# TensorE's order inside a unit of the first attention: score, logit, value products or piece, score, logit, rest

## The reference, cut to what matters

```
x_norm = layer_norm(x, g1, beta1)
q, k, v = x_norm @ Wq + bq, x_norm @ Wk + bk, x_norm @ Wv + bv     # 16 heads of 8
q, k = apply_rope(q) / sqrt(8), apply_rope(k)
attn = softmax(q @ k.T);  out = attn @ v                            # per head, 512 x 512
x = x + out @ Wo + bo
x = x + relu(layer_norm(x, g2, beta2) @ W1 + b1) @ W2 + b2
```

## Time and profile before

| | |
|---|---|
| median of 3 runs | 1780.76 us (1778.65 to 1782.49) |
| span of the profiled execution | 1776.1 us |
| around the span, from the median | 4.7 us |
| mean granted TensorE clock | 0.912 |
| PE / PEld / DVE / ACT / POOL busy | 82% / 54% / 72% / 53% / 39% of the span |
| first attention, main loop | 54.7 to about 604 us |

### The profile page before, as it was taken

One profiled execution on the slowest core, in us unless ns is written; L12 is line 12 of the kernel. 1 busy time (PEld: TensorE's weight loads), 2 busy tenths in 40 slices (PEclk: granted clock), 3 DMA queues, 4 the chain that ended last, 5 costly groups with the idle time before them and its releaser, 6 DMA issues. The chain is left out here.

```text
span 1776.1 us, 37567 instructions
## 1 busy us (share of the span) xinstructions
PE 1455.7 (82%) x11726; PEld 964.8 (54%) x11726; DVE 1274.7 (72%) x3482; ACT 935.2 (53%) x1914; POOL 694.1 (39%) x812
## 2 busy tenths in 40 slices
PE   3999999999999729995378887878888887837993
PEld 1224334333343319994256766666666665627993
DVE  6777888888787435555777879697978786834555
ACT  2577777777775505662435455454545453314561
POOL 3122342633520334554233344444444541233552
PEclk8699999999998969997689999898999998978997
DMA  6211111111110332222544443434344434132225
GB/s 158 66 42 59 47 52 53 61 53 49 49 62 15 128 123 67 73 72 82 164 150 126 126 128 106 131 109 129 112 125 122 130 111 138 38 130 56 71 72 162
DMA packets 122418, 166.37 MB, mean 94 GB/s; under 512 B 21490, under 2 KB 96018, under 8 KB 121586
## 3 DMA queue, kind: packets, MB, share of 16 engines
q1 hardware_dynamic: 113330, 145.69, 28.1%
q0 software_dynamic: 8896, 18.30, 3.0%
HBM read 116.04 MB, written 47.60 MB: 92 GB/s over the span
## 5 line engine op out<-in xcount | busy, mean ns | idle before, releaser
L1124 DVE TENSOR_REDUCE a_M<-a_F 128x1 f32<-128x512 f32 x512 | 325.8, 683 | 90.0 <-PE a_F L1318 88.1
L1025 ACT ACTIVATE L_W<-a_ST 128x512 f32<-128x512 f32 x512 | 276.8, 595 | 89.1 <-PE a_ST L1359 88.3
L2028 ACT ACTIVATE L_W<-c_ST 128x1024 f32<-128x1024 f32 x160 | 163.3, 1021 | 188.4 <-PE c_ST L2408 141.1
L2630 ACT ACTIVATE L_hT<-L_P,L_W1s 128x128 f32<-128x128 f32 x600 | 171.5, 368 | 142.9 <-PE L_P L2711 110.6
L2616 POOL DMA_INDIRECT L_yd<-L_ys,L_di x150 | 163.1, 1087 | 151.6 <-DVE L_ys L2662 147.2
L489 POOL DMA_INDIRECT L_xd<-L_XN,L_place_i x128 | 124.4, 972 | 146.5 <-issue 131.9
L1359 PE MATMUL a_ST<-L_W 74*128 74x512 bf16 x512 | 168.9, 395 | 11.1 <-ACT L_W L1025 6.3
L1318 PE MATMUL a_F<-L_W 72*128 72x512 bf16 x512 | 167.1, 403 | 7.7 <-DVE a_M L1124 6.9
L2702 PE MATMUL L_P<-L_xT,L_W1s 128*128 128x128 f32 x1200 | 161.0, 278 | 0.0
L2711 PE MATMUL L_P<-L_W,L_hT 128*128 x1200 | 159.1, 276 | 0.1
L2407 PE MATMUL c_ST<-ident,c_SD 128*128 128x128 f32 x512 | 149.7, 292 | 5.5 <-ACT L_W L2028 5.5
(11 more groups left out here) (430 smaller groups left out, 3164.9 us busy)
## 6 DMA issues: line engine op xcount, KB each, us to landing
c_QS<-c_q SPq DMA_DIRECT2D x32, 504.0 KB
c_QS<-c_rd SPq DMA_DIRECT2D x32, 378.0 KB
L_xg<-L_xd SPq DMA_DIRECT2D x150, 64.5 KB
L_W<-a_q SPq DMA_DIRECT2D x32, 288.0 KB
L_W<-a_k SPq DMA_DIRECT2D x96, 96.0 KB
L_W<-c_k SPq DMA_DIRECT2D x96, 96.0 KB
L_W<-in_L_w SPq DMA_DIRECT2D x8, 1024.0 KB
c_QI<-c_r SPq DMA_DIRECT2D x32, 216.0 KB
```

What stands on the lines that cost most here:

```text
L1025: act.activation(PT[:, j, kk, :], ST[:, kk, :], ACT.Exp).then_inc(sem(exped), 1)
L1124: dve.tensor_reduce(M[:, t, h:h + 1], FB[n % BANKS][:, :], AX_X, ALU.max).then_inc(sem(maxed), 1)
L2028: act.activation(PT[:, j, :, :], ST[:, :, :], ACT.Exp).then_inc(sem(exped), 1)
L2630: act.activation(hT[:, n % 2, f, :], PS[2 + 2 * (n % 2) + f // 2][:, (f % 2) * P:(f % 2 + 1) * P], func, bias=W1s[:, n % WB, F + f:F + f + ...
```

## The change

Inside a unit TensorE's order was: score, score, [turn_max], logit, logit, [value products], [piece], [turn_values]. It becomes: score, logit, then the value products where the unit has them and the piece where it has none, score, logit, [turn_max], [the piece, in a unit that has value products], [turn_values]. `scores` issues one score instead of two. No instruction is added or removed, and the orders of ScalarE, VectorE, GpSimd and the DMA queues stay.

```
-            def scores(i, g, j):
+            def scores(i, g, j, kk):
...
-                if j == 0:
+                if j == 0 and kk == 0:
                     pe.wait_ge(*turn(mstacked, i, 32 * (g + 1)))
-                for kk in range(2):
-                    kt = 2 * w + kk
-                    pe.wait_ge(*turn(exped, i, 2 * (UQ * g + j) + kk - 1))
-                    pe.matmul(ST[:, kk, :], KS[0:KR0, h, kt * P:(kt + 1) * P], QS[0:KR0, h, :],
-                              start=True, stop=True).then_inc(sem(scored), 1)
+                kt = 2 * w + kk
+                pe.wait_ge(*turn(exped, i, 2 * (UQ * g + j) + kk - 1))
+                pe.matmul(ST[:, kk, :], KS[0:KR0, h, kt * P:(kt + 1) * P], QS[0:KR0, h, :],
+                          start=True, stop=True).then_inc(sem(scored), 1)
...
-                        scores(i, g, j)
+                        b, ns = ahead(i, g, j, n1) or (i, [])
+                        uses = pieces(u, tail, n1, n2, routed)
+                        valued_here = j in (5, 6) or (j in (1, 2) and (g or tail))
+                        scores(i, g, j, 0)
+                        for n in ns[0:1]:
+                            logits(b, n)
+                        if j in (1, 2) and g:
+                            values(i, g - 1, j + 1)
+                        elif j in (1, 2) and tail:
+                            values(i - 1, NQ - 1, j + 1)
+                        elif j in (5, 6):
+                            values(i, g, j - 5)
+                        else:
+                            for use in uses:
+                                piece(use, i, prev)
+                        scores(i, g, j, 1)
+                        for n in ns[1:2]:
+                            logits(b, n)
                         if j == 5 and has_quad(g, 1, n1):
                             turn_max(*next_quad(i, g))
-                        if ahead(i, g, j, n1):
-                            b, ns = ahead(i, g, j, n1)
-                            for n in ns:
-                                logits(b, n)
-                        if j in (1, 2):
-                            if g:
-                                values(i, g - 1, j + 1)
-                            elif tail:
-                                values(i - 1, NQ - 1, j + 1)
-                        if j in (5, 6):
-                            values(i, g, j - 5)
-                        for use in pieces(u, tail, n1, n2, routed):
-                            piece(use, i, prev)
+                        if valued_here:
+                            for use in uses:
+                                piece(use, i, prev)
```

## The result

The kernel after takes 1801.42 us, the median of 4 runs (1796.91 to 1813.03), where the kernel before took 1780.34 (1778.65 to 1782.49, 4 runs): a ratio of 1.0159, 95% interval 1.0102 to 1.0216. It is slower. The forecast was 1795, with a range of 1779 to 1812.

The account below looks back on a forecast made before the run. TensorE was taken to set the main loop's pace (busy 528.6 of 550 us), with short waits behind ScalarE and VectorE. Full batches, joints and batch 0 summed to +13.8 us on 1780.8, giving 1795, range 1779 to 1812.

Parts of the forecast that it names:

- pieces behind each other: Consecutive piece units: next piece waits for ScalarE's copy behind the second exponential; +0.64 units 15/16, +0.70 units 7/8.
- The +0.8 of units 31 and 0: Batch joint: the piece wait between units 31 and 0, claimed to cost 0.8 us.
- the normalisations: Later second exponential delays minus_max and XN by 0.68: net +0.42 from unit 21; YN +0.1, ZN -0.15.
- the joint: Between batches: second logits come later, so two 0.65 us waits for VectorE's maxima go, 1.3 us saved.
- units 19 and 20: Piece wait for ScalarE's copy, with turn_values between as partial cover: +0.28 us per full batch.
- units 2 to 4 at nothing: Units 2, 3, 4: extra waits and units 4 and 5's losses taken as 0, bounds -0.1 and +0.4.
- Batch 0: First batch, almost without pieces: 3.3 lost at quad joints, 1.1 and 1.2 gained, net +1.0 us.
- The landing of the quad's maxima: Later turn_max makes the maxima's DMAs land late in batch 0: 1.1 us at three quad joints, 3.3.
- The runs with less wait: Batch 0, five runs of units without value products or piece: spread scores avoid 0.2 us waits, estimated -1.1.
- the two waits for maxima: Batch 0: two waits for maxima like those at the batch joint were to go, -1.2 us.
- The clock, the rival of 0.14: Piece waits bring more 1.2 GHz stretches: 36 us more, 1831, or 1813 with half; chance 0.14.
- The faster case: Spread scores keep ScalarE from falling behind; all waits but the piece pairs' 2.9 go: 1771 us; chance 0.10.

Follow-up runs that it names:

- e3: Changed kernel, but ScalarE copies the piece of a unit without value products between that unit's two exponentials; 1830.93 us, ratio 1.0060 to the kernel before.
- e1: Changed kernel with every piece put back behind the second logit, value products staying between the pairs; 1826.9 us, ratio 1.0031 to the kernel before.
- e2: Changed kernel with units that have value products ordered as in the kernel before, pieces still moved in the others; 1852.56 us, ratio 1.0185 to the kernel before.
- e5: e3 plus ScalarE's quad-maxima copy, XN and YN between exponentials, and TensorE's turn_max directly behind the first logit; 1782.29 us, ratio 1.0066 to the kernel before.
- e6: e5 plus VectorE's other work of a unit between its two maxima; 1766.68 us, ratio 0.9942 to the kernel before; again 1762.39 us, 0.9924.
- f1: Changed kernel with only VectorE's edit of e6, its other work of a unit between the two maxima; 1836.97 us, ratio 1.0138 to the kernel before.
- r1: Kernel before, unchanged, profiled a second time in the second set of runs; 1781.51 us in one profile.
- r2: Changed kernel, unchanged, measured and profiled again in the second set of runs; 1795.47 us, ratio 1.0144 to the kernel before.
- e4: Changed kernel with VectorE's statistics of units 18 and 23 between the unit's two maxima; 1848.4 us, ratio 1.0172 to the kernel before.

## Why the prediction was right or wrong, point by point

Sums over batches 2 to 5 per batch, forecast and measured, in us:

| units | forecast | measured |
|---|---|---|
| 7 and 8 | +0.70 | +0.97 |
| 15 and 16 | +0.64 | +0.71 |
| 19 and 20 | +0.28 | +0.89 |
| 21 to 23 | +0.42 | +0.51 |
| 25 to 28 | +0.10 | +0.06 |
| 11 to 13 | -0.15 | -0.16 |
| 5 and 6 | 0 | -1.04 |
| 31, 0 to 4 | -0.7 | +2.5 |
| all | +1.3 | +4.5 |

- **Right: pieces behind each other.** Units 15 and 16, forecast from ScalarE's order by steps, came out to 0.07, and e3, which changes that order alone, takes the loss away. The +0.8 of units 31 and 0 shows as +0.71 in unit 0 at the first two joints and is covered by the late maxima at the others. Of the 0.97 at units 7 and 8, only 0.46 is the piece, where 0.70 was forecast. The other 0.51 is in unit 7, where neither e1 nor e3 changes anything. ScalarE's other work there (the split of a rotated row, L982, 0.62 us) stands behind the late second exponential of unit 6 as well; that this is the cause was read from the order and not tried.
- **Right: the normalisations.** +0.76 in unit 22, -0.25 in unit 23, together 0.51 against 0.42. e2 puts it back, and e5, which moves `minus_max` and XN ahead of the second exponential, brings unit 22 to 2.27.
- **Wrong: the joint.** "It now comes about 1 us later, so the two waits at the batch's joint go" is the step that failed. The statement on the logit was true, but it was held against maxima at their old times. VectorE's maxima at the joint are themselves queued behind routing statistics, whose start hangs on a chain that begins with statistics behind another late logit, eight units earlier. Both moved, the statistics of unit 23 from 0.19 us ahead of unit 24's first score to 0.81 behind it, and L348 with them. The clean comparison is e6 against e5, in one set: with VectorE's work between the two maxima the wait of unit 1 goes from 1.36 to 0.49 us. The wait of unit 31 stays (1.2 to 1.5 us in e6), so even with both lists matched the two waits do not go as forecast. Of the +2.5 of this row some 0.9 is the low clock, which had moved into units 2 and 3 (below).
- **Wrong in its mechanism: units 19 and 20.** I had counted a wait for ScalarE's copy (+0.28). What is there is a wait for a maximum, +0.89 in unit 20, which e3 leaves (2.75) and f1 and e6 remove but for 0.34 (2.23 and 2.22).
- **Wrong: units 2 to 4 at nothing.** Units 2 and 3 cost +1.6 together. About 0.9 of it is the low clock: units 2 and 3 take 3.74, 3.62 and 4.47 us where batches 4 and 5 fell to it, against 2.70 and 2.69, 3.7 us in four batches. The rest is order. In unit 2 I had looked for ScalarE's copies; e3 leaves it at 3.00, f1 brings it to 2.41. At the joint of batches 1 and 2, where neither the low clock nor an idle time disturbs it, it takes 3.03 after and 2.41 in f1, and the piece in it waits 0.40 us for VectorE's scaling (L371), which stands behind unit 1's second maximum. Unit 3 keeps 0.35 in every kernel whose pieces are moved (2.69 or 2.71; 2.34 in e1), and that was not followed further.
- **Batch 0: +1.9 against +1.0, by other ways.** The landing of the quad's maxima, forecast at 1.1 three times, cost nothing that shows: units 7, 15 and 23 grew by 0.39, 0.04 and 0, unit 8's first score waits for an exponential and not for the DMA, and in e5 and e6, where `turn_max` is early, unit 7 is longer still (1.73 against 1.56). The runs with less wait gave four times -0.25, about the forecast -1.1, but units 11 and 19 gave 0.3 each back. Units 5 and 6 cost +0.8, in a stretch at the low clock. Of the two waits for maxima one went, together with a low-clock stretch in the same unit (25: -1.95 us for both). The other grew from 0.55 to 1.40 us: units 20 and 21 cost +2.2, of which the +1.5 of unit 21 stands in and behind a stretch at the low clock (from 100.2). Unit 22, behind the normalisation, costs +0.79 here too, for which I had counted nothing.
- **The clock, the rival of 0.14: it went the other way.** The granted clock of the kernel before has seven stretches of 3.4 to 10.2 us at 0.50 in the loop behind its start, those of after four, with 17 us less of it in all (61 against 44, the first stretch included, 31 and 24 us). At half speed that gives back about 8 us, most of it in batches 6 and 7, which had four of the seven stretches before (20.5 us) and have none after: they are 5.0 us shorter where I forecast 4.0 longer. How much lies there is scatter of a profile: r1 has 6.8 us of it in these two batches and r2 none, and there the change costs 1.0 us. In batches 2 to 5 the level has 6.8 us before and 10.2 after (17.1 in r1, 6.8 in r2); it leaves unit 5 and turns up about 6.7 us into batches 4 and 5, so in units 2 and 3. By the Trainium skill ("TensorE: Matmul & The Clock Gate", A second HAM failure mode: psum-queue depth-cycling) short gaps between bunches of matmuls that go round PSUM banks make the clock swing. Here there were more such gaps, and longer ones, with the low level down from 61 to 44 us in the first pair of profiles; over the loop alone it went from 47.5 to 30.2 us, and from 43.0 to 20.4 in r1 and r2. This case does not bear the rule out.
- **The faster case** rested on the view that two scores apart cost ScalarE nothing. With its order matched this is nearly so: in e5 units 8, 16 and 0 are at 1.89, 1.97 and 1.90, and a piece wait of 0.25 us is left in unit 3. That this alone does not make the kernel faster (1.0066), VectorE's order does.

So the sign and the range held, and the size was near because errors of both signs met: in batches 2 to 5 the joints and units 19 and 20 cost 15 us more than forecast ((2.5 + 0.7 + 0.61) x 4, with 3.7 us of low clock in it), units 5 and 6 came out 4 shorter (3.1 of it low clock that had left them), and batches 6 and 7 together 9 shorter, which no term had. That they met is luck.

**What e6 wins.** Against the kernel before, its full batches are 1.04 us shorter. Units 5 and 6 alone give -1.28 (5.41 to 4.13, where the kernel before fell to the low clock), units 12 and 13 another -0.85; units 3, 7 and 20 give 1.19 back. In batch 1, where neither kernel's clock falls in these units, they take 4.63 before and 4.13 in e6, so -0.5 of the -1.28 is the order and some 0.8 the clock. So most of this gain is the clock: in batches 2 and 4, where the kernel before stayed at the full clock too, e6 is 0.42 us shorter (68.87 against 69.29, 69.25 against 69.67), in batches 3 and 5 it is 1.7 and 1.6. Over the loop e6 has 26.9 us at the low clock, and 13.5 in its second profile, against 47.5 and 43.0 before. Why the clock stays up with scores and logits in turns was not tried.

## What to carry to other kernels

When one engine's order is changed in a kernel whose engines each walk through a written list, the work of every reader that stands behind a moved result moves too. Go through each reader's list behind the moved result, down to the transfers and engines it feeds, before a wait is called gone: the same TensorE order was 1.5% slower with the readers' lists as they were, and 0.6 to 0.8% faster with both lists matched, most of which came with a clock that fell less often; one list alone was not enough, and the lists without the TensorE order cost 4%. Where two waits stand in one place, taking the longer away shows the other: judge such an edit by the lengths of units and not by the total. And where something else stops the engine just ahead of the place, the wait there says nothing of the edit.

## What the runs showed of the hardware

**Sets of runs.** The kernel before took 1770 and 1777 us in two sets and 1812 and 1822 in the two others. In the latter every kernel profiled (none of them the kernel before itself) had idle time in units 27 to 30 of batches 2 to 5, while GpSimd's gathers of the routing ran or just behind them, most of it with no releaser in the profile. The gathers themselves took no longer on GpSimd (0.98 us on average in e4 as in the kernel after). A row of PE of e4, then a window behind it, at the low clock, and a row of f1:

```profile
413.12 1.11 PE L1346 MATMUL a_TB<-ident,a_pvs 128*128 128x128 f32 x4 [2.06 <-issue]
```

```profile
415.00:420.00 5.00, 4.54 (x15) 0.86 (x13) 4.65 (x8) 2.15 (x4) 2.10 (x2) 0.50 0.08 26
```

```profile
337.15 0.45 PE L1359 MATMUL a_ST<-L_W 74*128 74x512 bf16 x1 [1.93 <-issue]
```

What it is stays open. That it belongs to a chip is not shown: the third set (1811.64) and the fourth (1776.76), some five minutes apart, are on record under the same chip number. It is a reason to compare kernels within one set, and to read the units outside this stretch.

**A releaser named that was not the cause.** PEld and PE, unit 8 of batch 2, kernel after:

```profile
213.61 0.10 PEld L1358 LDWEIGHTS a_ST<-L_W 74*128 74x128 bf16 x1 [0.87 <-DMA L_W<-a_less]
...
213.65 0.38 PE L1358 MATMUL a_ST<-L_W 74*128 74x512 bf16 x1 [0.40 <-ACT L_W L1025]
```

The weight load names the DMA with the quad's maxima, the matmul an exponential; both came within 0.1 us or so. In e5 and e6, where `turn_max` is early and no such DMA wait is named in this place, unit 7 is as long as here (1.89 and 1.87 against 1.87). The DMA cost nothing here. The trace puts 9.0 us in all on 11 weight loads that waited for it, seven of them at this place, one in each of batches 1 to 7.
